# Two projection chunks ahead of the weighted sum in place of one on either side, in a hybrid attention kernel with an FFN stage run twice

## The reference

```python
def attn_layer(x, Wqkv, qs, ksc, Wo):
    qkv = x @ Wqkv                       # 128 -> 3 x 1024, 16 heads of 64
    q, k, v = heads(qkv)
    q = l2norm(q) * qs;  k = l2norm(k) * ksc
    q = q * cos * scale + rotate_half(q) * sin * scale
    k = k * cos / scale + rotate_half(k) * sin / scale
    # windows of 32: each looks at itself and the one before, causal
    attn = softmax(where(mask, -big, q @ k.T * 8))
    return (attn @ v) @ Wo

for i in range(6):
    x = attn_layer(shift_tokens(x), ...) + x
    x = ffn_layer(shift_tokens(x), ...) + x   # layernorm, W1, a * gelu(gate), W2
```

## Time and profile before

| | us |
|---|---|
| Median of 3 runs | 3888.59 |
| Lowest, highest | 3873.29, 3900.0 |
| The profiled execution's own time | 3905.88 |
| Its span, first to last instruction | 3903.7 |
| PE busy | 3491.8 |
| DVE busy | 3004.6 |
| POOL busy | 2719.5 |
| ACT busy | 2710.9 |

### The profile page before, as it was taken

The page is one execution under the profiler, slowest core; times in us unless marked ns, Lnnn a source line. Parts: engine busy times, 40 slices in busy tenths (PEclk is TensorE's granted clock), DMA queues, the critical chain, the costliest instruction groups (busy, mean ns, idle before and its releaser), DMA issues. The chain is left out here.

```text
span 3903.7 us, 159146 instructions
## 1 busy us (share of the span) xinstructions
PE 3491.8 (89%) x62588; PEld 2485.2 (64%) x62588; DVE 3004.6 (77%) x4752; ACT 2710.9 (69%) x7080; POOL 2719.5 (70%) x3091
## 2 busy tenths in 40 slices
PE   8799999999999999985555789999999999999996
PEld 3577777777777777762111367777777777777774
DVE  7678788787787888855888778878778787778883
ACT  2478787787877787763434468777777777777874
POOL 4578787777787787850334478777778787777872
PEclk9899999999999999996778889999999999999998
DMA  1223332333333333320000023333333333332331
GB/s 40 61 69 77 76 83 69 83 75 73 80 72 79 78 75 77 78 53 16 0 0 0 21 68 77 77 81 73 76 73 76 75 76 74 80 76 68 88 71 37
DMA packets 183174, 252.07 MB, mean 65 GB/s; under 512 B 53659, under 2 KB 74783, under 8 KB 182303
## 3 DMA queue, kind: packets, MB, share of 16 engines
q1 hardware_dynamic: 182422, 241.71, 26.0%
HBM read 39.13 MB, written 1.05 MB: 10 GB/s over the span
## 5 line engine op out<-in xcount | busy, mean ns | idle before, releaser
L860 POOL TENSOR_TENSOR qk_rows<-rot_products 128x512 f32<-128x512 f32 x768 | 983.3, 1282 | 244.9 <-DVE rot_products L659 242.4
L659 DVE TENSOR_TENSOR rot_products<-psum,rot_scaled 128x1024 f32<-128x1024 f32 x768 | 937.4, 1221 | 162.1 <-ACT squares L470 117.9
L870 POOL TENSOR_TENSOR qk_rows<-qk_rows,rnorm 128x512 f32<-128x512 f32 x768 | 803.3, 1078 | 15.0
L266 PE MATMUL psum<-wqkv_hi,xs_hi 128*128 (+1 forms) x1152 | 561.9, 488 | 92.0 <-DVE rot_products L659 47.3
L470 ACT ACTIVATE squares<-psum 128x512 f32<-128x512 f32 x768 | 487.7, 635 | 73.5 <-PE psum L268 60.8
L661 DVE TENSOR_REDUCE sumsq<-squares 128x8 f32<-128x512 f32 x768 | 518.7, 675 | 0.0
L835 POOL TENSOR_TENSOR probs<-probs,rden 128x512 f32<-128x512 f32 x384 | 393.2, 1046 | 107.1 <-DVE rden L709 106.4
L514 ACT ACTIVATE probs<-psum,minus_row_max 128x64 f32<-128x64 f32 x1536 | 458.5, 336 | 5.9 <-DVE minus_row_max L693 5.8
L268 PE MATMUL psum<-wqkv_hi,xs_lo 128*128 (+1 forms) x1152 | 462.0, 401 | 0.0
L267 PE MATMUL psum<-wqkv_lo,xs_hi 128*128 (+1 forms) x1152 | 461.1, 400 | 0.0
L328 PEld LDWEIGHTS psum<-probs_t,v_pairs 64*64 64x64 f32 x24576 | 390.7, 136 | 106.7 <-issue 106.3
(11 more groups left out here) (159 smaller groups left out, 6081.7 us busy)
## 6 DMA issues: line engine op xcount, KB each, us to landing
v_pairs<-v_rows SPq DMA_DIRECT2D x3072, 64.0 KB
wqkv_staged<-in_Wqkv SPq DMA_DIRECT2D x52, 384.0 KB, 3.4
wo<-in_Wo SPq DMA_DIRECT2D x12, 512.0 KB, 4.2
w<-in_W SPq DMA_DIRECT2D x12, 341.0 KB, 3.2
qk_scale<-in_qk_scale SPq DMA_DIRECT2D x12, 128.0 KB, 3.2
w<-in_W SPq DMA_DIRECT2D x12, 128.0 KB
rot_base<-in_rot SPq DMA_DIRECT2D x2, 512.0 KB, 3.6
out_x<-qk_rows SPq DMA_DIRECT2D x1, 1024.0 KB, 5.7
```

Of the source, the lines that this page charges most:

```text
L266: nc.tensor.matmul(proj_ps[c % 2], xh, wh, start=True, stop=False)
L659: V.tensor_tensor(m["mm"][:, c % 2, :, :].rearrange("p a (h e) -> p a h e", e=DH), ps, cos_sin, ALU.mult)\
L860: G.tensor_tensor(qk[:, c * CH:(c + 1) * CH].rearrange(half, a=2, e=DH // 2), cos, sin[:, :, ::-1, :], ALU.add)\
L870: G.tensor_tensor(part, part, m["rn"][:, u % 2, HC * c:HC * c + HC].unsqueeze(2) .to_broadcast([P, HC, DH]), ALU.mult).then_inc(S["rot_don ...
```

## The change

In `pe_body`, chunk 1 of tile u+3 is issued right behind chunk 0, ahead of both halves of the weighted sum, and no longer behind them. Nothing else in the kernel is different, and no other engine's program.

```diff
--- before.py
+++ after.py
@@ -433,10 +433,9 @@
                 pe_pv_ready(it, u, mlp)
                 if ahead or u + 3 < TILES:
                     pe_proj(it, u + 3, 0, three)
+                    pe_proj(it, u + 3, 1, three)
                 pe_pv(it, u, 0)
                 pe_pv(it, u, 1)
-                if ahead or u + 3 < TILES:
-                    pe_proj(it, u + 3, 1, three)
 
         def pe_ffn(first):
             last, layer = first + PHASE - 1, first // B
```

## The result

The changed kernel takes 3912.64 us in the median of 10 runs (3903.21 to 3934.35), the kernel before 3887.85 us (3873.29 to 3900.51): ratio 1.0064, interval 1.0042 to 1.0086, some 25 us slower. Its profiled execution took 3910.19 us with a span of 3908.0. Lines behind the change are lower by one in its program (L268 is the same; L659 is now L658, L486 is L485, L478 is L477).

A forecast was written before the change was run, and what follows sets the result against it. PE's own queue was taken as the bound, busy 89% of the span. Terms 31 + 0 - 24 + 10 = +17 us on the 3888.6 us median gave about 3905 us, range 3860 to 3940.

The forecast's parts named there:

- (a), the stalls per slot: Chunk 1 waits for ACT to evict chunk 5: 0.17 us tile 3, 0.65 tile 0, 0.54 tile 1, 0 tile 2.
- (a), the cover: Stalls ahead of chunk 1 shorten PE's later waits at chunk 2 and o_t: 65 us uncovered becomes +31 us.
- (a), tile 1: A table load on ACT stalls chunk 1 by 0.54 us; 0.45 left after cover by the o_t wait, 22 us.
- (b): ACT's o_t eviction after the later-ending weighted sum: cost 0, bounds 0 and +5 us.
- (c), the holes: PE's stops inside the weighted sum, 27.2 us in 49 places; entered in the sum as -24 us.
- (d), the weight loads: Matmul weight loads of chunk 1 and of transposes now behind narrow matmuls: +0.05 us per slot, +10 us.
- 1: Chunk 1's stall counts whole, waits at chunk 2 and o_t don't shrink, holes unchanged: 3964 us, chance 0.13.
- 2: Holes in the weighted sum close and almost nothing is lost to stalls: 3857 us, 0.8% faster, chance 0.15.
- 3: Holes in the weighted sum stay, or new ones replace old: +41 us, 3930 us, chance 0.17.

The follow-up runs named there:

- shifted program: Kernel before with 60 more transposes (120 instructions) at the start of PE's program, loop order unchanged: 3895.71 us in one run.
- second comparison: The changed kernel, unaltered, timed again beside the kernel before on another chip: ratio 1.0069 (1.0046 to 1.0092).
- kernel without table loads: Gelu replaced by a square, so ACT loads no tables in the FFN stages: ratio to kernel before 0.9983 with the old order, 0.9984 with the changed order.
- mixed order with the early eviction: Against kernel before: chunk 1 between weighted-sum halves, but behind them in tile 0 and the loop's last slot; tile 0 evicts chunk 5 before ACT's weight copy: 0.9981.
- control: Kernel before, chunk 1 still behind the weighted sum, with only ACT's eviction of chunk 5 put ahead of its weight copy in tile 0: ratio 0.9993.

## Why the prediction was right, and where it was not

The forecast was +17 us, with no measurable change as the likeliest class; measured are +25 us, 0.64%, under the 1% named, and 3912.64 against 3905 forecast, inside 3860 to 3940. That it came out so near is luck: the terms of its sum were right in kind but come to about +4 us in the traces, and the larger part of the cost goes with PE's clock, for which the sum had no term. By its own steps:

- *(a), the stalls per slot*: 0.17, 0.65, 0.54 and 0 were forecast; 0.16, 0.47 and 0.53 are read in the rows above for tiles 3, 0 and 1. They come from ACT's rows and the hand-over of 0.06 us, which held to 0.01; in tile 0 ACT was earlier by 0.2 us, counted from chunk 0.
- *(a), the cover*: it held. Chunks with their waits took 42.2 us more and the output projection with its wait 20.5 less, so +22 net, where the sum had +31. The price of tile 0 can be read by itself: from the first transposes of the probabilities (L294) in one slot to those in the next, with chunk 2 and o_t inside, and in slots that stood wholly at 2.4 GHz, tile 0 takes 17.15 us before and 17.28 in the two executions of the changed kernel. These 0.13 us (standard error 0.14) go with the 0.1 forecast and not with the whole stall of 0.47.
- *(a), tile 1*: the same measure gives 15.51 and 15.63 us. The prediction called itself wrong if these slots do not grow by 0.2 to 0.5 us; they grew by 0.12 (standard error 0.07). The stall is there with its 0.53 us, but 13 of the 27 us of holes lay in tile 1 and closed, 0.27 us per slot, which the sign had left out.
- *(b)*: 0, and it held. The waits for o_t shrank.
- *(c), the holes*: 27.2 us of issue went to 1.7, and the shifted program shows that they are late blocks. From start to start the weighted sum takes 34 us less; a hole is 0.2 us longer than the page's idle time, since the modelled end of the matmul ahead of it covers its first part (the one of the earlier trace rows is 0.72 us from start to start). So the 24 was too small, and the bound of 27 with it.
- *(d), the weight loads*: +10 forecast; the transposes take 8.1 us more from start to start (12.3 by the page's busy time).
- *Missing, the branch*: moving chunk 1 takes the last wide work out of the loop's body and costs 28.5 - 21.6 = 7 us over six branches. That no queue lies behind the change's place but the branch was to be seen in the code.
- *Missing, the clock*: the sum priced every wait at its own length. In the second comparison the granted clock was lower by 0.0046 in the changed kernel's runs, which at the fitted 3.6 us for 0.001 is some 16 us, most of the cost. The terms alone, +22 - 34 + 8 + 8, make +4.

What stays open is why the clock falls: the pairs of waits in tile 0 were followed by a fall and lone waits of that length were not, but in the kernel without table loads the same pairs cost nothing. Of the rivals, 1 had a cost where the sum had almost none, but not its mechanism: the waits at chunk 2 and at o_t did shrink. 2 and 3 fell: the stalls are there, and the holes closed.

The rule of the Trainium skill that I weighed (Runtime: NRT & Kernel Launch, Instruction fetch mechanics: fetch is hidden, as the engine issues more slowly than its buffer fills) does not hold here: 49 holes, each ending 1.2 to 1.6 us behind a packet of q8, moved with the blocks' bounds. The same section says that a taken branch whose target is not in the current window of two pages forces a fetch before execution goes on. The trace agrees: 3.1 to 5.1 us of idle time behind each branch, with a packet of q8 in each of them.

The best version is the mixed order with the early eviction, 0.9981 (0.9964 to 0.9997), 0.2% under the kernel before and 0.8% under the changed one; from its control, 0.9993, the intervals do not tell it.

## What to carry to other kernels

A wait that is moved ahead of narrow work is priced by when its releaser ends, not by how much time it used to have; where the releasing engine has a copy or a table load in between, either put the eviction first or leave a stretch of work ahead of the wait. A change can cost more than the waits in the profile add up to, since PE's clock can be lower in its runs: look at the granted clock of each run, compare the kernels at equal clock, and only then price the waits. Add up from the start of one matmul to the start of the next, as modelled ends hide part of a wait. Keep something wide as the last work ahead of a loop's branch. Wide work ahead of a long run of narrow matmuls, or in its middle, gives late blocks time to arrive, but in the middle it pays for one more switch.

## What the runs showed of the hardware

- From the end of ACT's eviction to the start of the matmul that waits for it: 0.05 to 0.06 us.
